# Attention with unsplit probabilities: fp32 products in column groups, division inside the loop

## The chip, the cores and the metric

One NeuronCore of a Trainium2 chip runs the whole program. The metric is the device time of one execution in microseconds; the kernel before is given as the median of three executions.

## The reference, cut to what matters

The program has four layers on x of shape 16 images x 196 tokens (14 x 14) x 192 channels: a gated recurrent layer, an attention layer (l1), a mixture of experts, and a second attention layer (l3). Each normalizes by groups first and adds its result to its input. The change is in the attention layers. Of one, with 12 heads of 16 channels:

```python
attn = jnp.einsum('bqd,bkd->bqk', q * scale, k)
rel_h = jnp.einsum('bhwc,hkc->bhwk', qr, Rh)
rel_w = jnp.einsum('bhwc,wkc->bhwk', qr, Rw)
attn = attn + bias.reshape(B * nh, N, N)        # rel_h + rel_w
attn = jax.nn.softmax(attn, axis=-1)
out = jnp.einsum('bqk,bkd->bqd', attn, v)
...
return out @ proj_w + proj_b
```

## The kernel before, in words

All of it is in `attention_layer`, called for l1 and l3. Precision comes from splitting: a value is rounded to fp32r ("high"), the rest is its "low" part, and a product is made of high x high, low x high and high x low in single fp32r matmuls.

**Before the image loop** the layer makes q, k, v and the relative-position tables of the first four heads ("quad"), and writes q, k and the tables to device memory, from where each pair of heads is loaded in quarters.

**The image loop** has 96 images (six pairs of heads, 16 images each; an "image" is one image of one pair of heads) and runs as a software pipeline of steps i, the same on all engines (PE is TensorE, DVE VectorE, ACT ScalarE, POOL GpSimd, SP SyncE). In step i TensorE issues, in this order:
- `logits_by_query(i)` (L1159): four matmuls into two banks. They wait for `ml_ready`, VectorE's last instruction on the maxima of image i-1.
- `maxima_to_rows(i-1)` (L1168): four small bf16 matmuls that turn the maxima into two rows. ScalarE copies them into q (L1316).
- `rel` (L1144 to L1146), in 28 of the 96 steps: relative positions of the next quad through one bank. ScalarE takes the high part (L1290), VectorE the low part (L1353), and the next `rel` waits for that. Seven steps of fourteen read with a stride.
- `weigh_values(i-4)` (L1197, L1198): probabilities times values, eight matmuls: two heads x two halves of the keys x high and low part of the probabilities. The stationary side is a 66 column tile that holds both heads' values as high and low parts and a column of ones for each head, so that the sums of the probabilities come out with the products.
- `logits_by_key(i-1)` (L1180): four matmuls, which wait for L1316.

VectorE per step: the maxima of four blocks (L1388), two small instructions on them (L1393, L1395), the copy of the products (L1361) and of the two rows of sums (L1364), and L1353. ScalarE: L1316 and two exps of the same logits, one rounded to the high part (L1325) and one in full (L1328). GpSimd: the low part of the probabilities (L1080) and, for the next images, the split of the values (L1047, L1051).

**The sums.** Every two images a DMA stores the two rows (L935); every eight images ("an eighth" is eight images of one pair of heads, 12 in all) they are read back over 98 partitions (L942), inverted (L1368), split by GpSimd (L1059, L1061) and stored (L947).

**The end of a layer.** The reciprocals of all heads are read as 24 rows (L953), spread over the partitions of each head by matmuls with a 0/1 matrix `pick` (L1245), multiplied to the products by VectorE (L1411), split by ScalarE (L1335) and GpSimd (L1101), and projected with the split output weights in 12 matmuls per block and tile (L273), 8 tiles of 392 tokens. VectorE adds bias and input (L1422), in l1 it also takes the moments of the result for the next layer's normalization, and SP stores the tile (L1005). For l3 the output weights are split in the mixture already (L2055 and L1842); for l1 GpSimd splits them in the layer (L1024).

The order of SP's DMAs is written out by hand in `main_step(i)` and behind it. SP issues in order, so a DMA whose wait isn't met holds back all that follow.

## Time and profile before

| | |
|---|---|
| Time, three executions | 1790.2, 1793.58, 1793.66 us (median 1793.58) |
| Profiled execution: span (its own time) | 1796.6 us, 51708 instructions |
| TensorE matmul / weight load busy | 1485.9 us (83%) / 1272.1 us (71%) |
| VectorE / ScalarE / GpSimd busy | 1269.7 (71%) / 973.4 (54%) / 855.0 (48%) us |
| Mean granted TensorE clock | 0.802 of full speed |
| Image loop of l1: first and last query logits | 642.2 and 895.4 us |
| Image loop of l3: first and last query logits | 1483.3 and 1736.6 us |

Times in the views are microseconds from the span's start. No time is listed for the profiled execution beside its span. In a row of the order of time stand start, length, engine, line, operation, output and inputs, shapes and how many instructions were merged; in brackets the idle time before it and who ended it. PEld is the weight load, which lies beside matmuls. Matmul ends are modelled, so starts are compared, not ends. A clock of 1.00 is 2.4 GHz, 0.50 is 1.2 GHz.

### The profile page before, as it was taken

What the parts mean: (1) busy time and instruction counts of PE and PEld (TensorE: products, weight loads), DVE (VectorE), ACT (ScalarE), POOL (GpSimd) and SP (SyncE); (2) the same over time, 40 slices, a digit from 0 to 9 for tenths busy, and PEclk for the clock granted to TensorE, in tenths of its full rate; (3) what the DMA queues carried; (4) which work ended last, traced back from release to release, by engine and by line L of the source; (5) the groups of instructions that cost most, each with busy time, mean ns of one, the idle gap of its engine ahead of it and who ended that gap; (6) DMA issues with size and microseconds to landing.
All of it is one profiled execution on the core that took longest, in us unless ns stands there. A gap on an engine that the chain in (4) does not pass through costs nothing. (4 is left out here: it accounts for less than half of the span.)

```text
span 1796.6 us, 51708 instructions
## 1 busy us (share of the span) xinstructions
PE 1485.9 (83%) x19315; PEld 1272.1 (71%) x19315; DVE 1269.7 (71%) x4444; ACT 973.4 (54%) x1990; POOL 855.0 (48%) x1080
## 2 busy tenths in 40 slices
PE   4868888888876888889977999899998697888978
PEld 4757777777765776767755667678774586777766
DVE  7877787877778567879956684544446646888974
ACT  3633333333344567889924234555543556888972
POOL 2712222222235056879952111456551416787984
PEclk9955555555558889999986589899995798999998
DMA  3000000000002596667215204322225468666712
GB/s 87 1 20 4 4 5 4 4 4 4 4 3 83 171 257 151 147 156 161 58 48 173 98 24 151 125 81 86 83 73 153 144 159 254 166 147 150 146 29 58
DMA packets 72178, 165.21 MB, mean 92 GB/s; under 512 B 17938, under 2 KB 43162, under 8 KB 69436
## 3 DMA queue, kind: packets, MB, share of 16 engines
q1 hardware_dynamic: 66556, 149.05, 31.3%
q0 software_dynamic: 5376, 12.85, 2.3%
q8 instruction: 158, 2.59, 0.6%
q14 instruction: 88, 0.72, 0.1%
HBM read 93.84 MB, written 67.42 MB: 90 GB/s over the span
## 5 line engine op out<-in xcount | busy, mean ns | idle before, releaser
L1080 POOL TENSOR_TENSOR l_arena<-l_arena,l_arena 98x784 fp32r<-98x784 f32 x192 | 358.4, 1872 | 91.3 <-ACT l_arena L1328 79.0
L514 PE MATMUL gru_ps_r<-gru_hp,gru_wp 128*128 128x16 f16 x3920 | 200.1, 176 | 68.1 <-DVE gru_hp L489 68.1
L514 PEld LDWEIGHTS gru_ps_r<-gru_hp,gru_wp 128*128 128x128 f16 x3920 | 150.8, 106 | 88.5 <-DVE gru_hp L489 88.5
L567 POOL TENSOR_TENSOR gru_kept<-gru_keep,l0s_state 128x32 f32<-128x32 f32 x196 | 49.3, 251 | 305.4 <-ACT gru_keep L582 305.4
L1388 DVE TENSOR_REDUCE l_ps<-l_ps 98x4 f32<-98x784 f32 x192 | 187.5, 977 | 9.1 <-PE l_ps L1159 3.2
L514 PE MATMUL gru_ps_n<-gru_hp,gru_wp 128*128 128x16 f16 x3920 | 191.1, 174 | 0.0
L1197 PE MATMUL l_ps<-l_arena,l_arena 128*66 128x196 f32 x768 | 162.1, 264 | 20.9 <-POOL l_arena L1080 20.1
L580 ACT ACTIVATE gru_reset<-gru_ps_r,gru_unscale 128x32 f32<-128x32 f32 x196 | 56.4, 288 | 216.8 <-PE gru_ps_r L514 216.8
L1325 ACT ACTIVATE l_arena<-l_ps 98x784 fp32r<-98x784 f32 x192 | 158.4, 825 | 4.6
L1328 ACT ACTIVATE l_arena<-l_ps 98x784 f32<-98x784 f32 x192 | 157.0, 818 | 0.0
L1198 PE MATMUL l_ps<-l_arena,l_arena 128*66 128x196 f32 x768 | 155.0, 255 | 0.0
L514 PEld LDWEIGHTS gru_ps_n<-gru_hp,gru_wp 128*128 128x128 f16 x3920 | 150.0, 104 | 0.0
L1197 PEld LDWEIGHTS l_ps<-l_arena,l_arena 128*66 128x66 f32 x768 | 106.5, 139 | 41.0 <-POOL l_arena L1080 30.8
L1316 ACT ACTIVATE l_arena<-l_ps 2x392 fp32r<-2x392 f32 x192 | 94.1, 490 | 74.0 <-PE l_ps L1168 67.3
L1159 PE MATMUL l_ps<-l_arena,l_arena 128*98 128x196 f32 x768 | 110.7, 267 | 18.8 <-DVE l_mt L1395 13.7
L1159 PEld LDWEIGHTS l_ps<-l_arena,l_arena 128*98 128x98 f32 x768 | 85.6, 168 | 34.3 <-DVE l_mt L1395 25.3
L1198 PEld LDWEIGHTS l_ps<-l_arena,l_arena 128*66 128x66 f32 x768 | 107.0, 139 | 1.2
L1361 DVE COPY l_arena<-l_ps 64x196 f32<-64x196 f32 x192 | 67.7, 353 | 54.5 <-PE l_ps L1198 51.0
L1180 PE MATMUL l_ps<-l_arena,l_arena 128*98 128x196 f32 x768 | 103.5, 258 | 0.0
L1144 PE MATMUL l_ps<-l_arena,l_arena 128*56 128x224 f32 x168 | 59.8, 356 | 43.1 <-DVE l_arena L1353 40.4
L2231 DVE TENSOR_TENSOR l_arena<-mx_ps,l_arena 128x512 fp32r<-128x512 f32 x56 | 38.7, 692 | 77.9 <-ACT l_arena L2039 52.2
L1838 POOL DMA_INDIRECT picked<-l_arena,mx_target x56 | 55.3, 987 | 71.9 <-DVE l_arena L2238 60.5
(389 smaller groups left out, 4568.9 us busy)
## 6 DMA issues: line engine op xcount, KB each, us to landing
l_arena<-qk SPq DMA_DIRECT2D x96, 294.0 KB
qk<-l_arena SPq DMA_DIRECT2D x48, 392.0 KB, 9.0
rel<-l_arena SPq DMA_DIRECT2D x24, 686.0 KB
l_arena<-rel SPq DMA_DIRECT2D x48, 343.0 KB
qk<-l_arena SPq DMA_DIRECT2D x12, 784.0 KB, 7.9
l_arena<-in_experts_dram SPq DMA_DIRECT2D x8, 1152.0 KB, 7.6
l_arena<-x SPq DMA_DIRECT2D x24, 294.0 KB, 5.3
l_arena<-x SPq DMA_DIRECT2D x24, 196.0 KB, 3.1
```

What stands on the lines that cost most here:

```text
L514: last = pe.matmul(out[:, b, B * m:B * m + B], wp[:, wi, g, m, :], hp[:, b, part, B * k:B * k + B], start=False, stop=True, skip_group_che ...
L1080: pool.tensor_tensor(pl[g % LOWS][:TH, :, :], p32[:TH, g % 2, :, :], ph[:TH, g % 4, :, :].bitcast(f32), ALU.subtract).then_inc(pl_ready, 1)
L1144: pe.matmul(out, rh[:, n, :], line(high), start=True, stop=False)
L1159: last = pe.matmul(ps[:TH, S_BANK + head, half * T:half * T + T], q[:, head, queries], k[:, head, keys], start=True, stop=True)
L1180: last = pe.matmul(ps[:TH, T_BANK + 2 * (g % 2) + head, half * T:half * T + T], k[:, head, keys], q[:, head, queries], start=True, stop=True)
L1197: pe.matmul(out, values, ph[:, g % 4, head, cols], start=head == 0 and keys == 0, stop=False)
L1198: last = pe.matmul(out, values, pl[g % LOWS][:, head, cols], start=False, stop=head == 1 and keys == 1)
L1316: act.activation(q[0:2, :, b * T:(b + 1) * T], ps[64:66, R_BANK, :TB].rearrange("p (h t) -> p h t", h=2), ACT.Copy).then_inc(x_copied, 1)
L1325: act.activation(ph[:TH, g % 4, :, :], banks, ACT.Exp).then_inc(p_high, 1)
L1328: act.activation(p32[:TH, g % 2, :, :], banks, ACT.Exp).then_inc(p_ready, 1)
L1361: dve.tensor_copy(o_quad[p // 2][row:row + 64, b * T:(b + 1) * T], ps[:64, O_BANK, :T]).then_inc(o_kept, 1)
L1388: dve.tensor_reduce(m, ps[:TH, S_BANK:S_BANK + 2, :TB].rearrange("p c (h k) -> p c h k", h=2), AXIS.X, ALU.max).then_inc(mx_ready, 1)
```

## The change

1. The probabilities are one fp32 tile (one exp an image, four slots). The value tile is v itself, 16 columns and a column of ones per head; nothing is split. GpSimd loses L1080, L1047 and L1051, ScalarE L1325.
2. `weigh_values(n)` works on a pair of images, in the even steps from 4 on (a lag of 3). Eight fp32 matmuls with 17 stationary columns write four groups of output partitions (0, 32, 64, 96), one for each image and head of the pair, in one bank; the two key halves of a group follow each other. VectorE copies all 128 partitions at once, products and sums.
3. The division moves into the steps. Of each eighth the sums are stored, read back, inverted, stored and read again with each row broadcast over 16 partitions; GpSimd multiplies; four DMAs repack the quotients into rows as the projection wants them. For the twelfth eighth all this follows the loop.
4. At the end of the layer `pick`, L1245, L1411, L1335 and L1101 are gone. The projection is two fp32 matmuls per block and tile, of 128 and 64 rows, with unsplit weights that both layers load themselves.
5. In the mixture the split of l3's output weights goes (one DMA, one ScalarE and one GpSimd instruction).

Cut to its core (waits that only follow the renamed semaphores, placements and declarations left out):

```diff
-    LAG = 4
+    LAG = 3
...
+                def store_sums(h):
+                    sp.wait_ge(o_kept, 4 * h + 4)
+                    sp.dma_start(sums_dram[h]..., o_stage[h // 2][HD:128:32, ...]).then_inc(sums_stored, 16)
+                def load_spread(h):
+                    sp.wait_ge(rec_stored, 16 * (h + 1))
+                    if h < 2: sp.wait_ge(spread_zero, 1)
+                    else: sp.wait_ge(divided, h - 1)
+                    for j in range(4):
+                        row = rec_dram[h].rearrange("(j n) -> j n", j=4)[j:j + 1, :].to_broadcast([HD, EIGHT])
+                        sp.dma_start(spread[32 * j:32 * j + HD, h % 2, :], row).then_inc(spread_in[h % 2], 16)
+                def pack(h):
+                    sp.wait_ge(divided, h + 1)
+                    for j in range(4):
+                        ...
+                        sp.dma_start(place, eighth(h)[32 * j:32 * j + HD, :].rearrange("r (c t) -> r c t", c=4)).then_inc(packed[half], 16)
...
-                    g = i - LAG - 1
-                    if g >= 0 and g % 2 == 1:
-                        store_sums(g)
-                    if i >= 14 and i % 8 == 6:
-                        load_sums((i - 14) // 8)
-                    if i >= 21 and i % 8 == 5:
-                        store_reciprocals((i - 21) // 8)
+                    for at, act_on in ((11, store_sums), (13, load_sums), (17, store_reciprocals), (19, load_spread)):
+                        if i >= at and (i - at) % 8 == 0 and (i - at) // 8 < 2 * PAIRS - 1:
+                            act_on((i - at) // 8)
+                    if i >= 54:
+                        for h in range(2 * PAIRS - 1):
+                            if i == max(8 * h + 23, 54 + 2 * h):
+                                pack(h)
...
-                store_reciprocals(2 * PAIRS - 2)
-                load_sums(2 * PAIRS - 1)
-                sp.wait_ge(t_summed, IMAGES)
-                load_spread(0)
-                store_reciprocals(2 * PAIRS - 1)
-                load_spread(1)
+                pack(2 * PAIRS - 2)
+                last = 2 * PAIRS - 1
+                store_sums(last); load_sums(last); store_reciprocals(last); load_spread(last); pack(last)
...
-                    pool.tensor_tensor(pl[...], p32[...], ph[...].bitcast(f32), ALU.subtract).then_inc(pl_ready, 1)
+                for h in range(2 * PAIRS):
+                    pool.wait_ge(spread_in[h % 2], 64 * (h // 2 + 1))
+                    pool.wait_ge(o_kept, 4 * h + 4)
+                    pool.wait_ge(sums_stored, 16 * (h + 1))
+                    pool.tensor_tensor(o, o, spread[:, h % 2, :], ALU.mult).then_inc(divided, 1)
...
-                def weigh_values(g):
-                    out = ps[:66, O_BANK, :T]
-                    for head in range(2):
-                        for keys in range(2):
-                            pe.matmul(out, values, ph[:, g % 4, head, cols], start=..., stop=False)
-                            last = pe.matmul(out, values, pl[g % LOWS][:, head, cols], start=False, stop=...)
+                def weigh_values(n):
+                    p, c = divmod(n, B // 2)
+                    pe.wait_ge(p_ready, 2 * n + 2)
+                    if n >= 1:
+                        pe.wait_ge(o_kept, n)
+                    for j in range(4):
+                        for keys in range(2):
+                            e, head = divmod(j, 2)
+                            out = ps[32 * j:32 * j + VW, O_BANK, :T]
+                            values = v[:TH, 2 * (2 * c + e) + keys, 2 * p + head, :]
+                            last = pe.matmul(out, values, p32[:TH, (2 * n + e) % 4, head, keys * T:keys * T + T], start=keys == 0, stop=keys == 1)
+                    last.then_inc(o_summed, 1)
...
-                    if i >= LAG:
-                        weigh_values(i - LAG)
+                    if i >= LAG and (i - LAG) % 2 == 1:
+                        weigh_values((i - LAG) // 2)
...
+                    for m in range(CB):
+                        out = ps[:CP, 2 * (n % 2) + m, :TB]
+                        pe.matmul(out, wo[:, 0, m, :], o_full[0][:, cols], start=True, stop=False)
+                        pe.matmul(out, wo[:64, 1, m, :], o_full[1][:64, cols], start=False, stop=True).then_inc(y_summed, 1)
...
-                        act.activation(ph[:TH, g % 4, :, :], banks, ACT.Exp).then_inc(p_high, 1)
-                        act.activation(p32[:TH, g % 2, :, :], banks, ACT.Exp).then_inc(p_ready, 1)
+                        act.activation(p32[:TH, g % 4, :, :], banks, ACT.Exp).then_inc(p_ready, 1)
...
-                    dve.tensor_copy(o_quad[p // 2][row:row + 64, b * T:(b + 1) * T], ps[:64, O_BANK, :T]).then_inc(o_kept, 1)
-                    dve.tensor_copy(ring[:, slot, b % 2 * T:b % 2 * T + T], ps[64:66, O_BANK, :T]).then_inc(sums_kept, 1)
+                    dve.tensor_copy(o_stage[p][:, c * T:(c + 1) * T], ps[:, O_BANK, :T]).then_inc(o_kept, 1)
```

## Rows read from the trace of the kernel before

**Rows 1.** Busy time by stretch: VectorE's L1388 alone, then every engine

```profile
797.00:896.00 99.00, 43.35 (x45) 1.00 0.57 123
...
1747.00:1759.00 12.00, 4.04 (x10) 2.57 (x10) 3.68 (x8) 2.37 (x2) 3.27 (x4) 0.50 0.13 32
```

**Rows 2.** Order of time, VectorE, one plain step of the first attention layer

```profile
886.17 0.17 DVE L1395 TENSOR_TENSOR l_mt<-l_ps,l_mt 98x4 bf16<-98x4 f32 x1
886.36 0.35 DVE L1361 COPY l_arena<-l_ps 64x196 f32<-64x196 f32 x1
886.75 0.36 DVE L1364 COPY l_arena<-l_ps 2x196 f32<-2x196 f32 x1
887.14 0.98 DVE L1388 TENSOR_REDUCE l_ps<-l_ps 98x4 f32<-98x784 f32 x1
```

**Rows 3.** Order of time, TensorE and GpSimd, the plain step before it

```profile
883.94 0.60 PE L1159 MATMUL l_ps<-l_arena,l_arena 128*98 128x196 f32 x4
884.47 0.34 PE L1168 MATMUL l_ps<-l_ones_at,l_mt 98*2 98x98 bf16 x4
884.81 0.28 PE L1197 MATMUL l_ps<-l_arena,l_arena 128*66 128x196 f32 x1
...
885.46 0.25 PE L1198 MATMUL l_ps<-l_arena,l_arena 128*66 128x196 f32 x1
...
885.22 1.86 POOL L1080 TENSOR_TENSOR l_arena<-l_arena,l_arena 98x784 fp32r<-98x784 f32 x1
```

**Rows 4.** Order of time, VectorE, the reduces from 672 to 682 us

```profile
672.87 0.98 DVE L1388 TENSOR_REDUCE l_ps<-l_ps 98x4 f32<-98x784 f32 x1
...
674.94 0.98 DVE L1388 TENSOR_REDUCE l_ps<-l_ps 98x4 f32<-98x784 f32 x1
...
681.29 0.96 DVE L1388 TENSOR_REDUCE l_ps<-l_ps 98x4 f32<-98x784 f32 x1
```

**Rows 5.** Order of time, steps with relative positions: TensorE, then ScalarE and VectorE

```profile
755.16 0.32 PE L1144 MATMUL l_ps<-l_arena,l_arena 128*56 128x224 f32 x1 [0.49 <-DVE l_arena L1353]
...
758.28 0.32 PE L1144 MATMUL l_ps<-l_arena,l_arena 128*56 128x224 f32 x1 [0.49 <-DVE l_arena L1353]
...
783.98 0.39 PE L1144 MATMUL l_ps<-l_arena,l_arena 128*56 128x224 f32 x1 [0.78 <-DVE l_arena L1353]
...
787.91 0.39 PE L1144 MATMUL l_ps<-l_arena,l_arena 128*56 128x224 f32 x1 [0.78 <-DVE l_arena L1353]
...
785.44 0.96 ACT L1290 ACTIVATE l_arena<-l_ps 56x448 fp32r<-56x448 f32 x1
...
786.94 0.92 DVE L1353 TENSOR_TENSOR l_arena<-l_ps,l_arena 56x448 fp32r<-56x448 f32 x1
```

**Rows 6.** Order of time, the last image of the second attention layer

```profile
1736.32 0.61 PE L1159 MATMUL l_ps<-l_arena,l_arena 128*98 128x196 f32 x4
...
1746.94 0.36 DVE L1364 COPY l_arena<-l_ps 2x196 f32<-2x196 f32 x1
```

**Rows 7.** L520, fp32: its instructions (min/median/max ns), then in order of time

```profile
L520 PE MATMUL gru_ps_r<-l_arena,gru_most x2: 373/397/421, 94.7 to 94.8; 128*1 128x128 f32 x2
...
94.65 0.59 PE L520 MATMUL gru_ps_r<-l_arena,gru_most 128*1 128x128 f32 x2 [8.90 <-DVE gru_most L448]
```

**Rows 8.** Order of time, the end of the second layer: queue, VectorE and TensorE

```profile
1747.59 0.32 SPq L947 DMA_DIRECT2D rec<-l_rec_parts  x1
1748.60 0.31 SPq L942 DMA_DIRECT2D l_sums<-sums  x1
1749.09 0.29 SPq L953 DMA_DIRECT2D l_arena<-rec  x1
1750.14 0.35 DVE L1368 RECIPROCAL l_sums<-l_sums 98x32 f32<-98x32 f32 x1 [2.85 <-DMA l_sums<-sums]
...
1751.75 1.31 PE L1245 MATMUL l_ps<-l_arena,l_pick 24*128 24x392 f32 x3 [5.24 <-DMA l_arena<-rec]
```

**Rows 9.** L1033 of GpSimd: what it stood idle for (us, times)

```profile
  DMA rel<-l_arena: 58.4, 2
```

More of the change, by code:

```diff
@@ L738, in weights @@
         at, parts = AT_W, []
-        for dims in ((QUADS, CB, 128), (CB, C), (QUADS, CB, CP)):
+        for dims in ((QUADS, CB, 128), (CB, C)):
             for part in range(2):
@@ L761, in attention_layer @@
         xh, xl = arena.place(0, CB, N, dt=f32r) if padded is None else padded, arena.place(2 * N, CB, N, dt=f32r)
-        ph, p32, pl = arena.place(0, 4, 2, TB, dt=f32r), arena.place(N, 2, 2, TB), [arena.place(at, 2, TB, dt=f32r) for at in (N + 4 * TB, N + 6 * TB, AT_W + SLOTS * TB)]
+        p32 = arena.place(0, 4, 2, TB)
         rel_tiles = arena.place(2 * N, N, dt=f32r)
-        o_quad = [arena.place(at, N) for at in (3 * N, AT_QKB, AT_QKB + N)]
+        o_stage = [arena.place(at + half * (N // 2), N // 2) for at in (N, 3 * N, AT_QKB) for half in range(2)]
+        o_full = [arena.place(at, N) for at in (2 * N, AT_QKB + N)]
         x_raw, q = arena.place(AT_Q, CB, N) if x_here is None else x_here, arena.place(AT_Q, 2, N, dt=f32r)
@@ L767, in attention_layer @@
         k = arena.place(AT_K, 2, N, dt=f32r)
-        v = arena.place(AT_V, 2 * B, C)
+        v = arena.place(AT_V, 2 * B, HEADS, VW)
         qk_a, qk_b = arena.place(AT_QKA, 2, N, dt=f32r), arena.place(AT_QKB, 2, N, dt=f32r)
         w_raw, at = [], AT_QKB
-        for dims in ((QUADS, CB, 128), (CB, C), (28, 56), (QUADS, CB, CP)):
+        for dims in ((QUADS, CB, 128), (CB, C), (28, 56)):
             w_raw.append(arena.place(at, *dims))
             at += int(np.prod(dims))
-        pick_raw = arena.place(at, QUADS, 128)[:2 * HEADS]
         xy = arena.place(AT_QKA, CB, N)
-        ring = arena.place(AT_W, SLOTS, TB)[:2]
-        at, tail = AT_Q, []
-        for part in range(3):
-            tail.append(arena.place(at, 3 if part else 2, QUADS, TB, dt=f32r if part else f32))
-            at += (3 if part else 2) * QUADS * TB
-        hn, oh, ol = tail
-        spread = arena.place(at, N, dt=f32r)[:2 * HEADS]
+        spread = arena.place(AT_W, 2, EIGHT)
+        wo = arena.place(AT_WO, 2, CB, CP)
         rh, rl = arena.place(AT_REL, 28, 56, dt=f32r), arena.place(AT_REL + 28 * 56, 28, 56, dt=f32r)
@@ L947, in store_reciprocals @@
[L947 to L953 removed]
+                    sp.wait_ge(rec_ready, h + 1)
@@ L1064, in _ @@
-                pool.wait_ge(v_ready, 2 * B)
-                pool.memset(ph[CP:, :, :, :].bitcast(f32), 0.0).then_inc(ph_padded, 1)
-                pool.wait_ge(ph_padded, 1)
-                for low in pl:
-                    pool.memset(low[CP:, :, :].bitcast(f32), 0.0).then_inc(pl_padded, 1)
-                pool.wait_ge(pl_padded, LOWS)
-                for n in range(2):
-                    high, low = split_values(n)
-                    for head in range(2):
-                        high(head)
-                    for head in range(2):
-                        low(head)
@@ L1182, in logits_by_key @@
                     last.then_inc(t_summed, 1)
[L1184 to L1193 removed]
+                def weigh_values(n):
+                    p, c = divmod(n, B // 2)
+                    if n == 0:
+                        pe.wait_ge(ones_ready, 1)
+                        pe.wait_ge(o_cleared, 1)
+                    pe.wait_ge(p_ready, 2 * n + 2)
+                    if n >= 1:
+                        pe.wait_ge(o_kept, n)
+                    for j in range(4):
                         for keys in range(2):
[L1195 to L1198 removed]
+                            e, head = divmod(j, 2)
+                            out = ps[32 * j:32 * j + VW, O_BANK, :T]
+                            values = v[:TH, 2 * (2 * c + e) + keys, 2 * p + head, :]
+                            last = pe.matmul(out, values, p32[:TH, (2 * n + e) % 4, head, keys * T:keys * T + T], start=keys == 0, stop=keys == 1)
                     last.then_inc(o_summed, 1)
@@ L1671, in mixture @@
     l3_raw, spot = [], E * EXPERT
-    for dims in ((QUADS, CB, 128), (CB, C), (QUADS, CB, CP)):
+    for dims in ((QUADS, CB, 128), (CB, C)):
         l3_raw.append(arena.place(spot, *dims)[:])
@@ L2289, in build @@
         averages = [first.place(AT_AVERAGES, CP)[:CP], first.place(AT_AVERAGES + CP, CB, 2, 128)[:CP]]
-        ahead = dict(xh=first.place(0, CB, N, dt=f32r), weights=first.weights()[:4], avg=dict(avg=first.place(AT_AVG, CP)[:CP]))
+        ahead = dict(xh=first.place(0, CB, N, dt=f32r), weights=first.weights(), avg=dict(avg=first.place(AT_AVG, CP)[:CP]))
         gru_layer(nc, ins, ins["x"], scratch["x1"], x_sb, x_stored, moments, ahead)
@@ L2309, in selectors @@
     ident[:TH] = np.eye(TH)
-    pick = np.zeros((2 * HEADS, QUADS, 4, 32), np.float32)
-    for head in range(HEADS):
-        pick[[head, HEADS + head], head // 4, head % 4] = 1.0
-    return np.ascontiguousarray(np.concatenate([sel, ident], 1)), pick.reshape(2 * HEADS, QUADS, 128)
+    return np.ascontiguousarray(np.concatenate([sel, ident], 1))
 def lay_out_attention(tag, wqkv, bqkv, wo, bo, rel_h, rel_w):
```

254 lines of the change are left out of this document (73 added, 181 removed).

## The prediction

> **What bounds the kernel now.** I read four views, in this order.
>
> First the reduce of VectorE alone, by stretch [rows 1]. In the last third of the first attention layer's image loop the core takes 45 images in 99 us at a granted clock of 1.00, so a plain step is 2.2 us. The second layer shows the same.
>
> Second, the order of time in such a step. VectorE has no gap over 0.04 us: subtraction, product copy 0.36, sum copy 0.36, reduce 0.98, then the cast and the next subtraction, 2.18 us in all [rows 2]. GpSimd is nearly as full: 1.86 us for the low part of the probabilities [rows 3], and value splits in three of four steps. So VectorE and GpSimd share the bound, and TensorE is third. Below both lies a floor that the change leaves alone: the logits of an image wait for the maxima of the last, since there is one pair of banks. Reduce 0.98, cast and subtraction with their gaps 0.41, four matmuls with their hand-overs 0.67: about 2.06, and a step of 2.07 does stand in the trace, 672.87 to 674.94 [rows 4].
>
> Third, the 28 steps of a layer that also make relative positions: 14 take 3.12 us and 14, with strided reads, 3.93 us [rows 5]. Their loop goes through one bank: six matmuls, the eight products behind them, both copies, the low part, and again.
>
> Fourth, the end of a layer [rows 6]. From the last query logits to the end is 1796.6 - 1736.32 = 60.3 us, of which 11.0 pass to the end of the last copy (1747.30).
>
> **The change, part by part.** W is the time of the eight fp32 products of a pair of images; it decides the case.
>
> *Price of W.* An fp32 product is recorded as two instructions. For 128 columns at 1.2 GHz their union is 0.59 us and the second lasts 0.373 [rows 7], so the second starts 0.217 us after the first: 2 x 128 / 1.2 = 0.213. Each instruction streams its columns twice, the product four times. The eight fp32r products of an image start between 884.81 and 885.46 [rows 3], 0.093 us each at full clock, where 196 / 2.4 is 0.082. So an fp32 product of 196 columns is 4 x 0.082 = 0.33 to 4 x 0.093 = 0.37 us, and eight one behind the other are 2.61 to 2.97; I take 2.75. The sixteen fp32r products that they replace are 16 x 0.093 = 1.49.
>
> No two neighbouring matmuls of the trace write different column groups, so whether four groups run side by side is not in it. The bounds are W = 2.97 (nothing overlaps) and W = 2 x 0.345 = 0.69 (all four groups at once). The nearest row is L1168 [rows 3], whose two output columns leave the rest of the array idle and whose four matmuls still come one behind the other: I take the upper end, and 2.75 for the sum.
>
> The Trainium skill (TensorEngine Tiling (Array Packing), Key Properties) says that different tiles can run weight loads and matmuls in parallel. No run here shows it; by it alone W would be the lower bound. The same skill (TensorE: Matmul & The Clock Gate, Part 3) says that matmuls keep strict program order; the diff issues four instructions of one group in a row, so by both together only the last of a group could lie beside the first of the next.
>
> *A plain step with products* (i even, from 4 on). TensorE: query logits to maxima rows 0.53 (883.94 to 884.47), those and the turn to the products 0.34 (884.47 to 884.81), W, key logits 4 x 0.09 [rows 3]. The second turn, back to whole columns, costs between nothing and 0.2 (estimate: what the 0.34 holds beyond four short matmuls), so 1.24 to 1.44 + W. I use 1.25, as the 0.34 holds one turn already: 4.00 us. *Without products*: the floor, 2.07. VectorE gives up two copies of 0.36 an image for one a pair, ScalarE one exp, GpSimd the 1.86 and the splits; none of that goes below the floor.
>
> *Steps with relative positions.* With products the loop loses 8 x 0.09 and one copy of 0.38 and gains W: 3.12 - 1.10 + W = 4.8, and 3.93 - 1.10 + W = 5.6. Without products the strided ones become 1.46 (first matmul to ScalarE's copy) + 0.97 + 0.92 + 0.08 = 3.43 [rows 5], the others, by the same chain with shorter pieces, come near the floor: 2.2. Even steps are 5 of the 14 short ones and 6 of the 14 strided.
>
> *A layer's 96 steps.* Before: 68 x 2.218 + 14 x 3.12 + 14 x 3.93 = 249.5. After: 35 x 4.00 + 33 x 2.07 + 5 x 4.8 + 9 x 2.2 + 6 x 5.6 + 8 x 3.43 = 313.1. That is +63.6 a layer, **+127** for both. One step of 6.35 us (674.94 to 681.29 [rows 4]) is a strided one that also waits for loads; slower steps before it hide that and smaller waits at the loop's start, some 4.5 a layer: **-9**.
>
> *The end of a layer.* After the change the last exp ends at some 7 us behind the last query logits, the last W near 10, its copy at 10.4. SyncE's queue then holds, in order, the repack of the eleventh eighth and the store, load, store, broadcast and repack of the twelfth. Prices [rows 8]: a small store 1.5 (1747.59 to 1749.09), the sums' load 1.5 (1748.60 to 1750.14), a broadcast at least the spread's 2.66 (1749.09 to 1751.75), and 3.2 with four issues of 0.3; the division of 784 columns 1.9, as L1080; the repack like the broadcast. The eleventh eighth is repacked at about 12, the twelfth at 23.5. The projection is 32 fp32 products of 392 columns, 8 x 0.09 = 0.73 each: 23.4 us, and some 3 more at the low clock that TensorE gets after its idle time (0.50 from 1747 to 1759 us [rows 1]). It starts at 12 and ends near 38.4; the last add, the store and the rest of the program take 5.5 now and then. So 44 against 60.3: -16. The first layer's end has the same chain, so **-32**. The bounds are +26 more (32 x 1.3 us, low clock throughout) and -10 (the twelfth eighth early).
>
> *At no cost.* The zeroing of the bank and the ones lie before the loop, under GpSimd's waits of 58.4 us for the stores [rows 9]; so do the missing pick and the wo split. If that cover were gone they would cost 1 us a layer. In the mixture one ScalarE copy and one GpSimd subtraction go; I count nothing. SyncE's queue gets eleven DMAs per eight steps instead of six, some 0.35 us of issue each, in 16 us and more; beyond that they would delay the loads.
>
> *Sum*: 127 - 9 - 32 = +86 on the profiled execution's 1796.6, so 1882.6. That span is 3 us above the median of the three runs shown, so the time is **1880**.
>
> **The rivals.**
>
> *In order, with neighbours overlapping.* Of the 16 instructions of a W, three lie beside the one before: 13/16 x 2.75 = 2.23. 35 x 3.48 + 68.3 + 5 x 4.25 + 19.8 + 6 x 5.06 + 27.4 = 289, +39.5 a layer: 79 - 9 - 32 = +38, 1832. For it: only an overlap of different groups is needed. Against: no row shows one. If whole products rather than instructions overlap, five of eight remain, W = 1.72: 33 - 5 - 32 = -4, 1790.
>
> *All four groups at once: faster.* W = 0.69 falls under the floor; plain steps are 2.07, the others 2.7, 2.2, 3.5 and 3.43: 223 a layer, -53 for both, -32 at the ends: 1709. Its place is the products of a pair, and it decides as soon as W is below some 1.8, where the loops no longer lose more than the ends win. For it: four groups write separate partitions. Against: the fifth instruction would have to start before the second.
>
> *The ends give nothing back.* With the projection at the low clock throughout, the ends lose 5 each instead of winning 16, beyond what the waits leave open; the forecast becomes some 1920.
>
> That the change doesn't do what it says is no rival here: each part has its line in the diff.
>
> **How the numbers follow.** Serial products 0.44, in-order overlap 0.28, five of eight 0.08, all at once 0.17, other 0.03. The likeliest case's own range is 1850 to 1910: W from 2.61 to 2.97 is 13 us down and 20 up, the turn of 0.2 up to 14, the ends the rest. The in-order case lies at 1832 and the five of eight at 1790, so the range goes down to 1780; all at once is left out. Faster by over 0.2% (about what a measurement of this kernel can tell from no change): 0.17 and most of 0.08, 0.24. Within: 0.03. Slower: 0.73.
>
> **What would show it.** The reduces of plain steps alternate between 2.07 and 4.0 us (3.5 by the first rival, always 2.07 by the second). Among a pair's products the first instruction of a new group starts 0.16 to 0.18 us after the last of the old one; a start within a few ns is overlap. GpSimd does one division in eight steps, VectorE is below two thirds busy. The layer's end is about 44 us after the last logits, with 32 products recorded as 64 instructions. I am wrong if the steps with products are below 3.3 us, or if the ends don't shrink.

## The result and the profile after

The changed kernel took 1808.78 us in the median of 7 runs (1794.93 to 1810.3), the kernel before 1793.58 (1783.31 to 1800.85) beside it: a ratio of 1.0083, 95% interval 1.0055 to 1.0110. It is slower, as forecast, but by 15 us and not by 86. Both halves of the sum were wrong: the two image loops together are as long as before (0.9 us more, for the forecast's 118), and each layer's end is 8 us longer instead of 16 shorter. The profiled execution has a span of 1803.8 us.

First the products. The order of time on TensorE in one plain step with products:

```profile
886.46 0.57 PE L1097 MATMUL l_ps<-l_arena,l_arena 128*98 128x196 f32 x4
886.96 0.20 PE L1106 MATMUL l_ps<-l_ones_at,l_mt 98*2 98x98 bf16 x1
886.97 0.35 PE L1136 MATMUL l_ps<-l_arena,l_arena 98*17 98x196 f32 x2
887.00 0.29 PE L1106 MATMUL l_ps<-l_ones_at,l_mt 98*2 98x98 bf16 x3
887.07 0.98 DVE L1294 TENSOR_REDUCE l_ps<-l_ps 98x4 f32<-98x784 f32 x1 [0.76 <-PE l_ps L1097]
887.13 0.84 PE L1136 MATMUL l_ps<-l_arena,l_arena 98*17 98x196 f32 x14
887.91 0.60 PE L1118 MATMUL l_ps<-l_arena,l_arena 128*98 128x196 f32 x4
...
889.15 0.98 DVE L1294 TENSOR_REDUCE l_ps<-l_ps 98x4 f32<-98x784 f32 x1 [0.43 <-PE l_ps L1097]
```

L1097 is the query logits, L1106 the maxima rows, L1136 the products, L1118 the key logits. The sixteen instructions of a pair's products start within the 0.94 us from 886.97 to the key logits at 887.91. Four groups run side by side, and the first two instructions even start ahead of three of the maxima rows issued before them. The step is 2.08 us (887.07 to 889.15), the floor of [rows 4], where [rows 2] had 2.18.

Second, where the loops' gain went. Two waits of layer 1, each in the order of time (one row of ScalarE, the queue or VectorE, and the reduces around it); the row ahead of them is ScalarE's of the kernel before, at the first of the two places:

```profile
679.51 0.92 ACT L1290 ACTIVATE l_arena<-l_ps 56x448 fp32r<-56x448 f32 x1 [2.24 <-DMA rel<-l_arena]
```

```profile
671.26 0.98 DVE L1294 TENSOR_REDUCE l_ps<-l_ps 98x4 f32<-98x784 f32 x1 [0.43 <-PE l_ps L1097]
679.36 0.92 ACT L1212 ACTIVATE l_arena<-l_ps 56x448 fp32r<-56x448 f32 x1 [6.49 <-DMA rel<-l_arena]
681.14 0.97 DVE L1294 TENSOR_REDUCE l_ps<-l_ps 98x4 f32<-98x784 f32 x1
...
799.45 0.31 SPq L930 DMA_DIRECT2D l_sums<-sums  x1
...
800.82 0.98 DVE L1294 TENSOR_REDUCE l_ps<-l_ps 98x4 f32<-98x784 f32 x1 [0.43 <-PE l_ps L1097]
...
806.79 0.35 DVE L1272 RECIPROCAL l_sums<-l_sums 98x32 f32<-98x32 f32 x1 [4.59 <-DMA l_sums<-sums]
807.06 0.92 DVE L1294 TENSOR_REDUCE l_ps<-l_ps 98x4 f32<-98x784 f32 x1
```

The first one is the long step of [rows 4]. Before, the 13th reduce stood at 681.29, now at 681.14: ScalarE waits for the store of the relative height tile before it may overwrite it, and its copy starts at 679.36 where it started at 679.51. It stood idle for the store for 2.24 us before and for 6.49 now. The core comes 3.7 us earlier (671.26 against 674.94) and waits 3.5 longer: 9.88 against 6.35. The second wait is new. A load of sums, issued at 799.45, is waited for until 806.79, with a DMA share near 1, and VectorE's next reduce stands behind its reciprocal: 6.24 us from the 56th reduce to the 57th, where the kernel before has 2.40. The stretches at it and right behind it (length, busy TensorE, granted clock, DMA share, GB/s), and in a fence of its own one of the kernel before:

```profile
800.00:805.00 5.00, 3.69 (x42) 1.00 1.00 158
805.00:810.00 5.00, 1.40 (x8) 0.66 0.98 184
810.00:815.00 5.00, 4.59 (x36) 0.50 1.11 146
815.00:820.00 5.00, 4.42 (x37) 0.50 0.89 168
820.00:825.00 5.00, 4.40 (x50) 0.98 0.48 94
```

```profile
810.00:815.00 5.00, 4.98 (x51) 1.00 1.02 203
```

So a wait costs twice: its own step is 4.2 us longer than a plain one, and the five steps behind it take 2.4 to 3.3 us each, 3.4 us more in all, at a clock that had fallen to 0.50 in the idle time. Before, the clock was 1.00 in all five stretches. It is not only here. Over a whole loop TensorE is idle for longer than before (204.54 us busy of 251.10, before 219.96 of 253.30), and its mean granted clock is lower. Loop 1 of the kernel before, then loops 1 and 3 of the changed one:

```profile
642.20:895.50 253.30, 219.96 (x2032) 0.97 0.64 156
```

```profile
641.90:893.00 251.10, 204.54 (x2039) 0.90 0.74 173
1479.10:1735.60 256.50, 205.83 (x2040) 0.89 0.72 169
```

With two levels, a mean of 0.90 is a fifth of the loop at 0.50, some 50 us; 0.97 is some 15 us.

Third, the end. Projection products of layer 3 (two instructions each; min/median/max ns; first and last start), and two stretches of the projection:

```profile
L1182 PE MATMUL l_ps<-l_arena,l_arena x32: 861/900/967, 1748.7 to 1795.9; 128*96 128x392 f32 x32
L1183 PE MATMUL l_ps<-l_arena,l_arena x32: 857/912/966, 1750.2 to 1797.5; 64*96 64x392 f32 x32
1750.00:1755.00 5.00, 5.00 (x8) 0.50 0.14 43
1790.00:1795.00 5.00, 5.00 (x7) 0.50 0.18 50
```

The 32 products take 49.6 us, 1.55 each, at a clock of 0.50 from first to last although the views count TensorE as busy throughout. From the last start of the query logits to the end are 68.2 us, before 59.9 ([rows 6] counts from the first of the four matmuls, 60.3).

The whole, cut at the first and the last start of the query logits in each profile (us), for this and the kernels below. The time is the median, the four parts are those of the one profiled execution, which need not be a median one (for v1 and e8 it is the longest of all):

| kernel | time | loop 1 | between | loop 3 | end |
|---|---|---|---|---|---|
| before | 1793.6 | 253.3 | 587.8 | 253.4 | 59.9 |
| after | 1808.8 | 251.1 | 586.1 | 256.5 | 68.2 |
| e2 one group | 1906.5 | 310.0 | 581.0 | 305.2 | 67.6 |
| e3 packs behind | 1850.3 | 253.2 | 616.1 | 247.7 | 90.5 |
| e5 width tile apart | 1790.3 | 247.8 | 592.6 | 243.6 | 67.8 |
| v1 split projection | 1801.0 | 254.4 | 593.1 | 257.2 | 65.7 |
| v5 tile, split, held | 1772.4 | 246.1 | 582.1 | 243.1 | 60.0 |
| e8 full rows | 1752.8 | 256.5 | 563.7 | 259.6 | 41.8 |
| e9 full rows, tile | 1736.8 | 249.3 | 563.5 | 244.3 | 42.1 |
| v4 tile, split, full rows | 1739.9 | 241.1 | 571.4 | 243.0 | 41.9 |

### The profile page after: what moved, and what is told of

Same layout as the page of the kernel before. It is cut to its first block and busy times, and to the rows that moved or that the text cites. A ratio compares the mean times of both kernels' runs of the same rounds, so it can differ in the third digit from the quotient of the medians.

```text
span 1803.8 us, 49953 instructions
## 1 busy us (share of the span) xinstructions
PE 1471.1 (82%) x19107; PEld 1154.7 (64%) x19107; DVE 1142.2 (63%) x4110; ACT 815.6 (45%) x1779; POOL 420.2 (23%) x643
## 5 line engine op out<-in xcount | busy, mean ns | idle before, releaser
L514 PE MATMUL gru_ps_r<-gru_hp,gru_wp 128*128 128x16 f16 x3920 | 198.9, 176 | 67.8 <-DVE gru_hp L489 67.8
L1039 POOL TENSOR_TENSOR l_arena<-l_arena,l_arena 128x784 f32<-128x784 f32 x24 | 44.4, 1852 | 508.3 <-DMA l_arena<-rec 508.3
L1118 PE MATMUL l_ps<-l_arena,l_arena 128*98 128x196 f32 x768 | 122.8, 286 | 37.0 <-ACT l_arena L1236 37.0
L1118 PEld LDWEIGHTS l_ps<-l_arena,l_arena 128*98 128x98 f32 x768 | 92.9, 179 | 84.1 <-ACT l_arena L1236 67.6
L1097 PE MATMUL l_ps<-l_arena,l_arena 128*98 128x196 f32 x768 | 119.3, 281 | 29.9 <-DVE l_mt L1301 22.6
L1097 PEld LDWEIGHTS l_ps<-l_arena,l_arena 128*98 128x98 f32 x768 | 91.8, 180 | 51.9 <-DVE l_mt L1301 39.4
L1261 DVE TENSOR_TENSOR l_arena<-l_ps,l_arena 56x448 fp32r<-56x448 f32 x84 | 64.8, 773 | 68.1 <-ACT l_arena L1212 67.1
L1136 PE MATMUL l_ps<-l_arena,l_arena 98*17 98x196 f32 x1536 | 103.5, 360 | 1.8 <-ACT l_arena L1243 1.8
L1212 ACT ACTIVATE l_arena<-l_ps 56x448 fp32r<-56x448 f32 x84 | 62.4, 743 | 49.8 <-PE l_ps L1084 34.1
L514 PE MATMUL gru_ps_z<-gru_hp,gru_wp 128*128 128x16 f16 x1960 | 81.1, 174 | 0.0
L528 PE MATMUL gru_ps_r<-l_arena,gru_ident 128*128 128x32 bf16 x588 | 68.2, 188 | 6.7 <-DVE gru_ident L477 6.7
L582 ACT ACTIVATE gru_keep<-gru_ps_z,gru_unscale 128x32 f32<-128x32 f32 x196 | 56.4, 288 | 37.6 <-PE gru_ps_z L514 37.6
```

What stands on the lines that cost most here:

```text
L514: last = pe.matmul(out[:, b, B * m:B * m + B], wp[:, wi, g, m, :], hp[:, b, part, B * k:B * k + B], start=False, stop=True, skip_group_che ...
L528: pe.matmul(ps_r[:, b, :2 * B], ident[:, :], gates_in[:, t, p, 2:4, :], start=p == 0, stop=p == 2, skip_group_check=True)
L1097: last = pe.matmul(ps[:TH, S_BANK + head, half * T:half * T + T], q[:, head, queries], k[:, head, keys], start=True, stop=True)
L1118: last = pe.matmul(ps[:TH, T_BANK + 2 * (g % 2) + head, half * T:half * T + T], k[:, head, keys], q[:, head, queries], start=True, stop=True)
L1136: last = pe.matmul(out, values, p32[:TH, (2 * n + e) % 4, head, keys * T:keys * T + T], start=keys == 0, stop=keys == 1)
L1212: act.activation(rel_out(r, 0), rel_sums(r), ACT.Copy).then_inc(rel_high, 1)
```

## The experiments

Times are medians; ratios are to the kernel before on the same chip (1790.1 us beside e1 to e4, 1791.2 beside e5, e6, v1 and v3, 1791.0 beside e7, v4, v5 and v6, 1789.4 beside e8, e9 and v7). e1, e2, e3, e4 and e7 were timed once each; a single time of the changed kernel can lie anywhere between 1794.9 and 1810.3 us.

### How the groups overlap: e1, e2

```diff
 e1   for keys in range(2):        # in place of: for j ... for keys
          for j in range(4):
 e2   out = ps[:VW, O_BANK, :T]    # in place of ps[32 * j:32 * j + VW, ...]
      dve.memset(ps[:, O_BANK, :], 1.0)    # in place of 0.0
```

> The products of a pair in the other order: first key half of all four groups, then the second. Theory A (column groups run side by side whatever the order, each group takes its next instruction when it is free): the 16 instructions of a pair stay within some 0.9 us, plain steps stay at 2.08, the time within 0.3% of the changed kernel's 1808.8. Theory B (only the order in a row lets them overlap): the 16 instructions need 2.6 us, steps with products 4.0, time over 1870. Theory C (strict order, a faster start with alternating groups): they shrink to 0.7 and nothing else moves, since the steps are at their floor.

> All eight products of a pair write the same column group (partitions 0 to 16), so that none can lie beside another; the sums of the other groups are set to one. What it leaves out: the products of three of four image-and-head pairs are lost, the work of every engine stays. It measures the serial price of W. My prediction's step: W = 2.6 to 3.0, steps with products 4.0, loops 60 us a layer longer than with W below the floor, time 1808 + some 90 less what waits absorb, 1870 to 1900. If fp32 products in a narrow group stream faster than four passes (rival), W stays near 0.85 to 1.3 and the time near 1810.

e2 writes all four products into group 0; it leaves out the results of three groups, whose sums are set to one. e1 took 1802.55 us, e2 1906.47. In e1's trace a pair's products take 0.91 us (887.62 to the key logits at 888.53), so the order of the key halves is worth nothing (theory A); the separate groups are worth some 98 us. A step of e2, in order of time:

```profile
935.89 0.34 PE L1136 MATMUL l_ps<-l_arena,l_arena 98*17 98x196 f32 x1
...
935.98 0.98 DVE L1294 TENSOR_REDUCE l_ps<-l_ps 98x4 f32<-98x784 f32 x1 [0.70 <-PE l_ps L1097]
936.07 2.65 PE L1136 MATMUL l_ps<-l_arena,l_arena 98*17 98x196 f32 x15
938.65 0.60 PE L1118 MATMUL l_ps<-l_arena,l_arena 128*98 128x196 f32 x4
...
939.65 0.98 DVE L1294 TENSOR_REDUCE l_ps<-l_ps 98x4 f32<-98x784 f32 x1 [0.54 <-PE l_ps L1097]
```

Serial, W is 2.76 us (935.89 to 938.65), the forecast's 2.75, and the step is 3.67 against its 4.00. The loops are 57 and 52 us longer than before, the forecast's +63.6 nearly. The price was right for products that come one behind the other; those of the changed kernel don't.

### The waits in the loops: e3, e5, e6, v7

```diff
 e3   pack(h) for all h after the loop, none in the steps
 e5 + rel_w1 = arena.place(3 * N, N, dt=f32r)    # second quad's width tile
      if r >= 2 * REL and r % 7 == 0:            # ScalarE waits for a store from here on,
                                                 # in place of r > REL
 e6   reciprocals, store, spread, pack of h < 9 three steps later
 v7   v4, and later by 3 (h to 6), 2, 1, 0, 0 steps
```

> The eleven repacks move from the image loop to behind it, the rest stays. Theory A (the stalls of 6.2 and 6.7 us at step 51 and the longer first steps of the last third come from SyncE's queue and the DMA engines, filled by the repacks): both stalls go, each loop is 4 to 8 us shorter, and the end of each layer grows by 11 x 2.6 = 28 us or so; total some 1850. Rival (the stalls are the q, k and table loads' own, as at step 12): the loops keep their length within 1 us, total some 1860.

e3 took 1850.28 us. In layer 1 its 56th reduce interval is still 5.57 us (6.24 with the packs) and the loop 2 us longer; in layer 3 the interval is 3.61 (6.66) and the loop 9 us shorter. The first is nearer the rival, the second theory A, and one profile each can't tell the packs' part from the loops' own spread: e1, whose order of products changes nothing, has 5.61 and 4.39 us there. What is sure is that the stall of layer 1 does not need the packs. Behind the loop they cost much:

```profile
901.25 28.63 SPq L955 DMA_DIRECT2D l_arena<-l_arena  x44
```

44 issues of 0.65 us stand ahead of the last eighth's store, on the path of the projection: the end is 22.3 us longer than the changed kernel's.

> The second group's width tile of the relative product gets a place of its own, so that ScalarE's copy of product 7 at step 12 no longer waits for the store of the height tile (in the changed kernel the 12th interval of the reduces is 9.88 us in layer 1 and 11.13 us in layer 3, and both kernels reach the 13th reduce of layer 1 at 681.1 to 681.3 us). Theory A, that this one wait gave back what the first twelve steps had won: the interval falls to 3.5 to 4.5 us and the kernel loses 5 to 8 us a layer, 10 to 15 us in all, against the changed kernel. Rival B, that the queue is simply full up to about 680 us and the next thing that it carries is late in its turn: a new stall of 3 us or more stands within the next six steps, or at step 16 where pair 1's first quarter is wanted, and the kernel is within 4 us of the changed one.

e5 took 1790.32 us, ratio 0.9993 (0.9972 to 1.0014), 18 under the changed kernel. The order of time around the same step:

```profile
671.77 0.94 ACT L1215 ACTIVATE l_arena<-l_ps 56x448 fp32r<-56x448 f32 x1
...
673.57 0.96 DVE L1299 TENSOR_REDUCE l_ps<-l_ps 98x4 f32<-98x784 f32 x1
```

ScalarE waits for no store, the 13th reduce is at 673.57, the interval 3.42 us. Theory A holds for this wait, and the medians give a little more than its 10 to 15 us. The two profiles divide it unevenly: loops 1 and 3 are 3.3 and 12.9 us shorter, as in loop 1 a later interval, the 64th, is 5.20 us in e5 and 2.81 in the changed kernel.

> The reciprocals of the first nine groups, with their store, spread and packing, come three steps later, so that VectorE no longer stands with a reduce behind a load of sums that was issued two steps before (6.24 us at the 56th interval in layer 1, 6.67 in layer 3, with 4.59 us idle for that load). Theory A, that VectorE's order makes the stall: the interval falls to 2.1 to 3 us, the one at step 64 (3.96 us in layer 3) to about 2.1, and the kernel comes out 5 to 12 us under the changed one. Rival B, that the loads of pair 3 and 4 themselves are late: the stall moves to the first query logits of the next quarter and the kernel is within 3 us of the changed one.

e6 took 1818.94 us, ratio 1.0159 (1.0131 to 1.0187), 10 over the changed kernel: a miss. The 56th interval fell to 2.14 us as theory A has it, but a new wait stands where the shift ends, with a step of 7.4 us (8.4 in layer 3):

```profile
883.39 0.35 DVE L1280 RECIPROCAL l_sums<-l_sums 98x32 f32<-98x32 f32 x1 [5.71 <-DMA l_sums<-sums]
```

By the code, the one tile of sums is loaded again only after the store of the last reciprocals, which the shift had moved up to just before it; no run isolates that. v7 lets the shift run out slowly, on top of v4.

> v4 with the reciprocals of groups 0 to 6 three steps later, group 7 two and group 8 one, so that no load of sums stands behind a store of the step before. If VectorE's order behind that load makes the stall, the intervals of 5.89 and 6.00 us at the 56th reduce fall to 2.1 to 3 us with no new one over 4 us, and it comes out 4 to 8 us under v4, at 1732 to 1736. If the transfers are late whatever waits for them, a stall of the same size stands somewhere behind it and the time is v4's within 3 us, or above it as in e6.

v7 took 1747.59 us, ratio 0.9771 (0.9744 to 0.9798), 8 over v4 where 4 to 8 under it were expected: again the 56th interval is gone (2.14 us), and again a wait of 4.62 us for sums stands further on (836.63), with a step of 6.3. In both runs VectorE's place behind the load moved the wait and did not take it away. What makes that load late is not settled; the DMA share beside it is near 1 in the changed kernel, and no run lightens the DMA engines there.

### The projection and the clock: e4, v1, v3, e7, v4, v5, v6, e8, e9

```diff
 e4 + for n in range(160): pe.matmul(ps[:TH, R_BANK, :TH], ones_at[:TH, :], ones_at[:TH, :], ...)
 v1   per part (128 and 64 rows): woh*oh, wol*oh, woh*ol in fp32r
      # oh by ScalarE, ol by VectorE (part 0) and GpSimd (part 1)
 v3   v1 with e5 and e6
 e8 + pool.memset(o_full[1][64:, :], 1.0)
    - pe.matmul(out, wo[:64, 1, m, :], o_full[1][:64, cols], ...)
    + pe.matmul(out, wo[:, 1, m, :], o_full[1][:, cols], ...)
 e7   e8 with e4's fillers
 e9   e8 with e5
 v4   e5 with v1, GpSimd's first low rows earlier, e8's 128 rows
 v5   v4 with 64 rows in part 1, 190 fillers
 v6   v4 with 190 fillers
```

> 160 small bf16 matmuls into a free bank before the projection, so that TensorE does not idle there and its clock is at 1.00 when the projection starts. Theory A (a stream of fp32 products leaves or brings the clock at 0.50 whatever was before): the clock falls within the first products, the projection takes 1.55 us a product as before, the time stays within 0.3%. Rival (it stays low because it starts low): the projection runs at 1.00, 0.78 us a product, 25 us a layer less, time some 1760.

e4 took 1803.62 us. Its stretches (length, TensorE busy, granted clock, DMA share, GB/s):

```profile
1745.00:1750.00 5.00, 2.86 (x15) 0.86 0.15 27
1750.00:1755.00 5.00, 5.00 (x7) 0.50 0.21 40
```

The fillers end some 2 us before the first product (1747.58). The projection is reached at 1.00, the clock falls to 0.50 about 1 us into it, and stays there to the end with TensorE counted as busy. I took that for a property of fp32 and split the products.

> The projection keeps its two products over 128 and 64 rows, but each as three fp32r products of high and low parts, which ScalarE, VectorE and GpSimd make as the tiles come in. Theory A, that the fp32 stream costs twice over, by its two instructions of 0.775 us a product and by a clock that stays at 0.50 through it, with TensorE busy all the time: the 12 products of a tile, 96 in all, take 0.37 us each at 0.50 and about 0.20 at full clock, so some 25 to 33 us in place of 49.6, and the clock rises above 0.50 before the end of the projection; with two layers the kernel comes out 25 to 45 us under the changed one, at 1765 to 1785. Rival B, that the end hangs on the chain of sums, reciprocals and packing and on the splits: the second half of the tiles is ready at about 12 us after the first, and the projection takes 40 us or more; the kernel is less than 12 us under the changed one. Rival C, that the clock is held at 0.50 at the end for whatever is done: 96 products of 0.37 us, 36 us, 25 us less in all, with 0.50 in every window.

> The width tile apart, the later division and the split projection together. If the three act in different places they add up: 10 to 15, 5 to 12 and 25 to 45 us under the changed kernel, 1740 to 1765 us, faster than the kernel before by 2% or more. If the transfers as a whole bound the loops, only the projection counts and the time is that of the split projection alone, within 5 us.

v1 took 1800.99 us, ratio 1.0041 (1.0017 to 1.0066), v3 1794.73, 1.0013 (0.9994 to 1.0032): 8 and 14 under the changed kernel where 25 to 45 and 44 to 69 were expected, both misses. v3 is 4 us over e5 alone, and e6's late division is in it. v1's three-term products took 39 us in each layer (1767.8 to 1806.5 in layer 3), all at 0.50, which is rival C's clock. Its end was 65.7 us, only 2.5 less than after: the stream is 10 us shorter and starts 8 us later, 21.0 us behind the last query logits for 13.1. v3's trace shows such a delay: the first product came 8 us after ScalarE began with the first tile (1747.85 against 1739.90), right behind GpSimd's low rows. But the kernel before has three-term products over 128 rows, and its own projection (from 1758.9) came back to 1.00:

```profile
1760.00:1765.00 5.00, 5.00 (x21) 0.73 0.00 0
1765.00:1770.00 5.00, 5.00 (x28) 1.00 0.21 60
```

So the next four turned to the rows.

> 160 small bf16 products hold TensorE busy from its last key logits to the projection, as in e4, and the second fp32 product of each pair takes all 128 rows in place of 64 (rows 64 to 127 are ones against weights of zero). Theory A, that the fp32 stream itself lets the clock fall (in e4 it was at 1.00 until 1747.5 us and at 0.50 from 1750 on, in a stream that was never idle): the clock is at 0.50 in every window of the projection again, which takes 49 to 50 us, and the kernel is at 1795 to 1812 us. Rival B, that the half filled rows let it fall: the clock stays at 1.00 and the projection takes some 25 us.

> The width tile apart and the split projection, with GpSimd's low rows moved ahead of its wait for the last spread (in v3 the first product waited until 1747.85 us, 7 us after its tile was packed), and 128 rows in every product. In v1 and v3 TensorE was busy all the time from 1750 to 1787 us at a clock of 0.50, where the kernel before, with 128 rows in its projection products, came back to 1.00 after 1763 us. Theory A, that a stream of whole 128-row products lets the clock rise: it is at 1.00 some 10 to 15 us after the projection's start, the 96 products take 22 to 30 us, and the kernel comes out at 1755 to 1775. Rival B, that the rows have nothing to do with it and the products' gaps (0.41 us each in v3, where 0.33 is what the third of each three takes) do: 0.50 throughout, 39 us, and 1780 to 1792 us, by the width tile and the earlier start alone.

> The same with products over 128 and 64 rows, and 190 small bf16 products between the last key logits and the projection, so that TensorE comes to it at a clock of 1.00. Theory A, that fp32r products keep a clock that they find, whatever their rows: 1.00 through the projection, 96 products of 0.20 us, some 20 us or what the second half's readiness leaves, and 1750 to 1768 us. Rival B, that 64-row products let it fall as the fp32 stream did in e4: 0.50 within 5 us of the start, 39 us again, and 1780 to 1795 us.

> Both: 128 rows in every product and a clock that is held until the projection begins. If either helps, this one has it: the projection at 1.00, some 20 us long, and 1750 to 1765 us, under the kernel before by 1.5 to 2.5%. If the clock falls here too, it falls for three-term products as such, and the kernel is at 1780 to 1795 us.

e7 took 1762.55 us, v4 1739.91 (0.9714, 0.9697 to 0.9731), v5 1772.38 (0.9891, 0.9876 to 0.9906), v6 1747.67 (0.9775, 0.9743 to 0.9806). v4 came out 15 us under its theory's range and v5 8 under its rival's, whose clock it has. The stretches of e7 (fp32, 128 rows), v5 (fp32r, 64-row products, reached warm) and v4 (fp32r, 128 rows, reached cold), one fence each:

```profile
1730.00:1735.00 5.00, 3.08 (x12) 1.00 0.14 24
1750.00:1755.00 5.00, 5.00 (x17) 1.00 0.37 110
```

```profile
1725.00:1730.00 5.00, 2.85 (x37) 0.97 0.07 12
1730.00:1735.00 5.00, 5.00 (x13) 0.50 0.17 40
1760.00:1765.00 5.00, 5.00 (x14) 0.50 0.22 66
```

```profile
1710.00:1715.00 5.00, 4.28 (x13) 0.50 0.17 43
1715.00:1720.00 5.00, 5.00 (x27) 0.91 0.19 34
1720.00:1725.00 5.00, 3.74 (x22) 1.00 0.60 167
```

With 128 rows in every product the clock is at 1.00, with 64 in every second block it is at 0.50, in fp32 and fp32r, reached warm or cold: e7 differs from e4 in the 64 added rows alone (and the ones written into them). Fillers bring nothing on top: v6 is 8 us over v4, and in layer 3 its clock fell to 0.50 twice, for some 3 us each. What remained was the edit by itself.

> The changed kernel with one edit: the second fp32 product of each pair in the projection takes 128 rows, of which rows 64 to 127 are ones against weights of zero; no fillers, nothing split. Theory A, that the 64-row products keep the clock at 0.50 (49.6 us in the changed kernel; with fillers and 128 rows it stayed at 1.00 in e7): it rises some 10 us after the projection's start, a pair of instructions takes 0.78 us in place of 1.55, the projection takes 30 to 36 us, and the kernel comes out 28 to 40 us under the changed one, at 1768 to 1780. Rival B, that an fp32 stream that starts at 0.50 stays there whatever its rows, and e7 had its clock from the fillers alone: 49 to 50 us, and 1800 to 1812.

> The same with the width tile apart. The two lie in different stretches, so they add up if theory A holds: another 10 to 15 us less, 1755 to 1768, and the split projection of v4 (1739.9) is worth the 16 to 20 us between, since its 96 products at full clock are 18 us against 25 for 32 fp32 ones. If the transfers of the end (packing of the second half of the tiles) bound both, e9 comes within 5 us of v4.

e8 took 1752.76 us, ratio 0.9784 (0.9756 to 0.9811). Its products of layer 3 and its stretches:

```profile
L1187 PE MATMUL l_ps<-l_arena,l_arena x32: 492/492/937, 1734.2 to 1756.6; 128*96 128x392 f32 x32
1730.00:1735.00 5.00, 0.76 (x2) 0.50 0.22 43
1735.00:1740.00 5.00, 5.00 (x12) 0.70 0.18 42
1740.00:1745.00 5.00, 5.00 (x16) 1.00 0.11 19
```

The projection takes 23.5 us from a start at 0.50; "between" and "end" are 22.4 and 26.4 us shorter than after. That is 49 of the 56 us between the medians (theory A expected 28 to 40); the profiled execution, with loops 8.5 us longer, is the longest of e8's seven (1747.56 to 1764.99).

Not all of it is the clock. The projection in the order of time at a clock of 0.50 on both sides, two rows of TensorE and one of a weight load, of the changed kernel and then of e8:

```profile
1750.22 1.62 PE L1183 MATMUL l_ps<-l_arena,l_arena 64*96 64x392 f32 x2
1751.77 1.62 PE L1182 MATMUL l_ps<-l_arena,l_arena 128*96 128x392 f32 x2
1751.77 0.39 PEld L1182 LDWEIGHTS l_ps<-l_arena,l_arena 128*96 128x96 f32 x2 [1.16 <-issue]
```

```profile
1735.63 1.51 PE L1188 MATMUL l_ps<-l_arena,l_arena 128*96 128x392 f32 x2
1736.93 1.36 PE L1187 MATMUL l_ps<-l_arena,l_arena 128*96 128x392 f32 x2
1736.28 0.28 PEld L1187 LDWEIGHTS l_ps<-l_arena,l_arena 128*96 128x96 f32 x1 [0.37 <-issue]
```

A product takes 1.55 us where 128 and 64 rows take turns and 1.30 where all have 128, at the same clock. In e8 the weights of a product begin to load 0.65 us before it starts (1736.28 for 1736.93), in the changed kernel at its start (1751.77), so that the load is not hidden behind the product before. That is 0.25 us a product, 8 of the 26 us that the projection became shorter; the other 18 are the clock. It also opens a rival that no run tests: in every projection that stayed at 0.50 the row count changed from block to block, and no run has 64 rows in all products. Whether the clock stays down for the few rows or for the turns is open. The edit removes both.

e9 took 1736.75, ratio 0.9697 (0.9660 to 0.9735), 16 less, about what the tile gave in e5, and equal to v4 within their intervals: with the clock up, the split buys nothing, where the expectation gave it 16 to 20 us. e9 is the changed kernel with two small edits, 3% under the kernel before.

## Why the prediction was wrong, step by step

**"I take the upper end, and 2.75 for the sum."** This is the step that failed: it took the products for serial and put W, the time of a pair's eight products, at 2.75 us. W is 0.94. The argument from L1168 [rows 3] was that four matmuls with idle columns come one behind the other; but those all write the same two partitions, as e2's products write the same seventeen, and e2 confirms the serial price to 0.01 us. That different tiles run side by side was the rule that the prediction quoted from the Trainium skill (TensorEngine Tiling (Array Packing), Key Properties), and the trace agrees with it: W is 0.94 us, for a lower bound of 0.69 and 2.76 measured in one group. The second rule that it quoted from the Trainium skill (TensorE: Matmul & The Clock Gate, Part 3), strict program order, gave 2.23 with an overlap at the seams only; here L1136 starts at 886.97, ahead of maxima rows issued before it that start at 887.00, and the measurement decides. "All four at once" had a chance of 0.17 and deserved most.

**The steps.** With W at 0.94 the rival's floor came out: plain steps 2.07 to 2.14 where nothing waits, short ones with relative positions 2.50 and 2.88 (2.2 and 2.7 were forecast), strided ones mostly 3.3 to 3.8 (3.43 and 3.5). The fixed part of a step with products was too large: in e2 it is 3.67 - 2.76 = 0.91 us for 1.25, and in the changed kernel the products start before the last maxima rows do.

**The loops.** The rival gave 223 us for 96 steps; measured are 251.1 and 256.5. The steps at the floor are there, the time is not. I counted a wait as something that slower steps hide (-9) and did not turn it round: faster steps uncover it. The wait for the height tile's store keeps its end (681.1), and so takes back all that the first twelve steps win; e5 gets it out, 18 us in the median. The wait for sums, which I had costed as SyncE's issues only, is new, with steps of 6.2 and 6.7 us. And the clock, which the sum left at 1.00 in the loops, is at 0.50 for a fifth of them. Of the 28 us between 223 and 251.1 in loop 1, the 12th interval (9.88 for 3.43) and the 56th with its five slow followers (20.1 for 12.5) are 14; the rest lies in many steps of 2.5 to 4 us and was not taken apart.

**The end.** The chain was right but for the projection. The changed kernel's first projection product starts 13 us behind the last query logits, for the forecast's 12. "0.73 each: 23.4 us, and some 3 more at the low clock" is nearly what e8 has, 23.5 us, and its end of 41.8 us is the forecast's 44. In the changed kernel the clock never rises, 1.55 us a product and 49.6 us. The prediction had this as a bound ("+26 more") and as the rival "the ends give nothing back", whose price was not the same: 5 lost each instead of 16 won is 42 for both. By its own terms the end would be 12 + 32 x 1.3 + 5.5 = 59 us, 1 won each. Measured are 8.3 lost each: the stream starts 1 us later, and the 1.3 us are the price in a stream of one row count (1.30 in e8 at 0.50); the turns add 0.25 a product, 8 us. With the end's +8.3, "between" -1.7 and the loops -2.2 and +3.1 the spans differ by 7.2 (0.3 is ahead of the first loop); the medians by 15.

So two of the forecast's terms, +127 and -32, were each wrong by more than the result. In the profiles the loops missed their term by 117 us one way (+1 for +118), the ends by 49 the other (+17 for -32). That the measured time still lies within the stated range of 1780 to 1910, and above the kernel before, is luck: the likeliest case's own range was 1850 to 1910, and what made the kernel slower are the layers' ends, for which the forecast had -16 each. The first layer's end is as much longer (last query logits to last projection product 55.1 us before, 63.4 after), and some 10 us between that and the third layer's loop gave it back. The starts of the same matmuls place most of them in the experts' products of the mixture: the changed kernel is 4.8 us behind at their start (1180.8 for 1176.0) and 4.6 ahead at their end (1352.1 for 1356.7). Which edit does it was not tested.

## What to carry to other kernels

Before a stall is called hidden, ask what the wait itself ends at: if a store or a load sets that time, faster steps only arrive earlier at it. Where every second product of a long stream leaves half the rows of TensorE empty, look at the granted clock in that stream and at the spacing of its starts; filling the rows (ones against zero weights) cost one memset here and took the kernel from 0.8% over the kernel before to 2.2% under it, 3.0% with one tile moved. And price column groups that write separate partitions at the lower bound as well as the upper, since that one factor was some 100 us.

## What the runs showed of the hardware

Eight fp32 products with 17 stationary and 196 moving columns take 0.94 us in four column groups and 2.76 in one; the order of the key halves does not matter (0.91 us in e1). Streams of 392-column products in which blocks of 128 and of 64 rows took turns sat at 0.50 for 38 to 50 us, in fp32 (after, e4) and fp32r (v1, v5); where they were reached at 1.00 (e4, v5, layer 3) the clock fell about 1 us after their start, some 2 us of idle time and 1 us of products behind the fillers. With 128 rows in all of them it rose from 0.50 to 1.00 within 4 to 6 us of the start (e8, e9, v4) or stayed at 1.00 (e7, layer 3). An fp32 product of 392 columns took 0.66 us at 1.00 and 1.30 at 0.50 in a stream of 128 rows (e8), and 1.55 at 0.50 where the row count took turns (after), where a product's weights begin to load at its start and not 0.65 us ahead of it. Whether the clock stays down for the few rows or for the turns, and why, no run here shows.
